# Two state tiles instead of three to TensorE's sum, a third full-size adding DMA, twelve state tiles, and products spread over the steps

## The reference, cut to what matters

```python
u = silu(causal_conv4(xc) + b_conv)          # xc, res = x @ W_in.T, 1024 channels each
dt, B, C = split(u @ W_xproj.T)              # 32, 16, 16
delta = softplus(dt @ W_dt.T + b_dt)
h_t = exp(delta_t * A) * h_(t-1) + delta_t * B_t * u_t     # 1024 channels x 16 states
y_t = sum over the 16 states of h_t * C_t
out = ((y + u * D) * silu(res)) @ W_out.T
```

## Time and profile before

| what | us |
|---|---|
| median of the runs | 2595.19 |
| the profiled execution, its span | 2590.08, 2588.0 |
| TensorE (PE) busy | 2419.2, 93% |
| VectorE (DVE) busy | 1823.6, 70% |
| GpSimd (POOL) busy | 1747.3, 68% |
| ScalarE (ACT) busy | 1442.7, 56% |

### The profile page before, as it was taken

The page is one execution under the profiler, slowest core; times in us unless marked ns, Lnnn a source line. Parts: engine busy times, 40 slices in busy tenths (PEclk is TensorE's granted clock), DMA queues, the critical chain, the costliest instruction groups (busy, mean ns, idle before and its releaser), DMA issues. The chain is left out here.

```text
span 2588.0 us, 38968 instructions
## 1 busy us (share of the span) xinstructions
PE 2419.2 (93%) x15744; PEld 1445.4 (56%) x15744; DVE 1823.6 (70%) x2154; ACT 1442.7 (56%) x2200; POOL 1747.3 (68%) x976
## 2 busy tenths in 40 slices
PE   6899999999999999999999998787999999999997
PEld 3465666665666666666666666543455554554543
DVE  3887897898798799789789878751465455355443
ACT  3577577667667757757757766631333433333332
POOL 0799898999999989989989999960332233143130
PEclk9999999999999999999999999998999999999998
DMA  4767866956866876786695685745000000000000
GB/s 140 191 129 144 223 143 132 235 130 150 218 137 143 190 178 139 163 204 139 142 238 131 140 210 124 155 87 205 1 1 33 33 22 12 33 33 1 17 17 17
DMA packets 158834, 309.23 MB, mean 119 GB/s; under 512 B 39232, under 2 KB 102208, under 8 KB 136000
## 3 DMA queue, kind: packets, MB, share of 16 engines
q0 software_dynamic: 27648, 167.78, 33.3%
q1 hardware_dynamic: 131008, 138.97, 16.3%
HBM read 119.57 MB, written 19.37 MB: 54 GB/s over the span
## 5 line engine op out<-in xcount | busy, mean ns | idle before, releaser
L851 POOL TENSOR_TENSOR mamba_ring<-mamba_ring,mamba_c_row 128x1024 f32<-128x1024 f32 x512 | 1268.1, 2552 | 98.2 <-DVE mamba_ring L748 94.8
L748 DVE TENSOR_TENSOR_SCAN mamba_ring<-mamba_ring,ps 128x512 f32<-128x512 f32 x1024 | 1179.4, 1203 | 189.1 <-PE ps L394 166.7
L602 ACT ACTIVATE mamba_ring<-mamba_delta,mamba_a_neg 128x512 f32<-128x512 f32 x1024 | 658.7, 712 | 85.5 <-DMA mamba_ring<-mamba_ring 84.4
L394 PEld LDWEIGHTS ps<-mamba_diag_b,mamba_v_t 64*128 64x128 f32 x8192 | 500.6, 188 | 291.8 <-issue 208.4
L394 PE MATMUL ps<-mamba_diag_b,mamba_v_t 64*128 64x128 f32 x8192 | 588.0, 285 | 45.7 <-DVE mamba_ring L748 44.3
L298 PE MATMUL ps<-mamba_xt,mamba_wu 128*128 128x512 f32 x512 | 253.4, 623 | 30.1 <-DMA mamba_wu<-w_u 16.1
L1519 POOL TENSOR_TENSOR xf_pr<-xf_pr,xf_top 128x1232 f32<-128x1232 f32 x32 | 75.0, 2343 | 277.2 <-DVE xf_top L1437 277.2
L356 PE MATMUL ps<-mamba_xt,mamba_wres 128*128 128x512 f32 x512 | 252.1, 615 | 0.0
L417 PE MATMUL ps<-mamba_ident,mamba_ring 128*128 128x128 f32 x1536 | 186.3, 278 | 23.6 <-DMA mamba_ring<-mamba_ring 23.5
L867 POOL DMA_DIRECT2D mamba_ring<-mamba_ring x192 | 175.1, 912 | 42.2 <-POOL mamba_ring L851 37.6
L1512 POOL TENSOR_TENSOR xf_xn<-xf_xn,xf_bo_s 128x512 f32<-128x512 f32 x32 | 39.5, 1268 | 222.8 <-PE xf_ps L1089 222.8
(11 more groups left out here) (114 smaller groups left out, 2939.5 us busy)
## 6 DMA issues: line engine op xcount, KB each, us to landing
mamba_ring<-mamba_ring POOLq DMA_DIRECT2D x128, 1024.0 KB, 7.8
mamba_c_row<-c_rows SPq DMA_DIRECT2D x32, 1024.0 KB, 12.2
mamba_ring<-mamba_ring POOLq DMA_DIRECT2D x64, 512.0 KB, 7.2
mamba_wu<-w_u SPq DMA_DIRECT2D x64, 256.0 KB, 3.1
mamba_wres<-w_res SPq DMA_DIRECT2D x64, 256.0 KB, 2.9
mamba_diag_b<-b_diagonals SPq DMA_DIRECT2D x56, 256.0 KB, 8.0
mamba_xt<-x_t SPq DMA_DIRECT2D x8, 1024.0 KB, 8.4
mamba_xres<-x SPq DMA_DIRECT2D x32, 256.0 KB, 4.3
```

The lines of the kernel that those rows point to most:

```text
L394: m = nc.tensor.matmul(ps[:, 2 * s + i, tb * P:(tb + 1) * P], v_t[g % 2][i * H:(i + 1) * H, tb * P:(tb + 1) * P], diag_b[i * H:(i + 1) * H ...
L602: a = nc.scalar.activation(ring[:, q % NR, i, :], delta[:, d, :], ACT.Exp, scale=a_neg[:, d, 2 * k + i:2 * k + i + 1])
L748: m = nc.vector.tensor_tensor_scan(ring[:, r, i, :], ring[:, r, i, :], both[:, bass.ds(i, T, 2)], 0.0, ALU.mult, ALU.add)
L851: nc.gpsimd.tensor_tensor(ring[:, q % NR], ring[:, q % NR], c_row[:, 2 * k:2 * k + 2, :], ALU.mult).then_inc(c_done, 1)
```

## The change

- `merge`: the third adding DMA sums tiles 4, 5 onto 6, 7 (1024 KB) and is issued at k = 1 of the next block; `SUMS` is (6, 7), summed at k = 6 of the next block, both behind `merged[2]`.
- The ring has twelve tiles, delta four blocks instead of eight; `DECAYS` gives its orders for k anew.
- y's transposes are at k = 7, `take_y` at k = 0 and the gating at k = 1 of the block after; v is made at k = 0.
- The parts of the gate, x and output products are spread over other steps, `dt_pair` goes to k = 2, the gate's and u's activations mostly to k = 0 of the next block, softplus to k = 3; `out_second` takes a list of blocks, uses other banks, and waits, adds and norms are moved with it. `dt_pair`, `v_transposes` and `u_product` get the waits that go with the new places (mostly not shown: `y_taken`, `vt_ready`, `delta_ready`, `z2_done`).

The diff, cut to its core; in the steps of TensorE and ScalarE the old lines are left out (they are in the functions above). `delta[:, d, :]` becomes `delta[:, d % EARLY, :]` in `softplus`, `decay` and `make_v`.

```diff
     NG = NB * ND
     TOTAL = NG * NU
     AHEAD = 3
-    DECAYS = ((3,), (), (4,), (5,), (6,), (7, 8), (9,), (10,))
+    DECAYS = ((3,), (4,), (5,), (6,), (7,), (), (8, 9), (10,))
     EARLY = 4
     FIRST_U = (0, 2, 4, 5, 6)
     TWO_U = (0, 1, 4)
     MOST = (5, 5, 6, 6)
-    NR = 10
+    NR = 12
     MERGES = 3
-    SUMS = (4, 5, 7)
-    FREED_BY_MERGE = {0: 0, 1: 0, 2: 1, 3: 1, 6: 2}
-    NEEDS_MERGE = {4: 1, 5: 1, 7: 2}
+    SUMS = (6, 7)
     NSUM = len(SUMS)
     BANK_A, BANK_B = 6, 7
...
         gate = [sb(f"gate{i}", [P, T]) for i in range(2)]
-        delta = sb("delta", [P, ND, T])
+        delta = sb("delta", [P, EARLY, T])
         diag_b = sb("diag_b", [P, TT, NU, H, 2])
         c_row = sb("c_row", [P, NS, T])
...
             def dt_pair(b, d):
-                if d == 4:
-                    pe.wait_ge(vt_ready, b * ND + 4)
-                    pe.wait_ge(y_taken, b * ND + 2)
-                elif d == 6:
-                    pe.wait_ge(y_taken, b * ND + 3)
-                    pe.wait_ge(vt_ready, b * ND + 5)
-                elif b >= 1 and d == 0:
-                    pe.wait_ge(xdbl_ready, b + 1)
-                    pe.wait_ge(y_taken, (b - 1) * ND + 5)
-                    pe.wait_ge(vt_ready, (b - 1) * ND + 7)
-                elif b >= 1:
-                    pe.wait_ge(vt_ready, (b - 1) * ND + 8)
-                    pe.wait_ge(y_taken, (b - 1) * ND + 6)
+                if b >= 1 or d >= EARLY:
+                    g = b * ND + d - 2
+                    pe.wait_ge(y_taken, g - 1)
+                    pe.wait_ge(vt_ready, g + 1)
+                    if d == 0:
+                        pe.wait_ge(xdbl_ready, b + 1)
+                    if d == 4 and b >= 1:
+                        pe.wait_ge(z2_done, (b - 1) * TT + 1)
                 for t0 in (0, T // 2):
                     for i in range(2):
...
                         pe.wait_ge(y_taken, g - 1)
-                    if d == 2:
-                        pe.wait_ge(delta_ready, b * ND + 5)
-                    elif d == 3:
-                        pe.wait_ge(delta_ready, b * ND + 8)
-                    elif d in (5, 6) and b + 1 < NB:
-                        pe.wait_ge(delta_ready, (b + 1) * ND + (2 if d == 5 else 3))
-                pe.wait_ge(merged[NEEDS_MERGE[k]], 16 * (g + 1))
+                    if d % 2 == 1 and (d != 5 or b + 1 < NB):
+                        pe.wait_ge(delta_ready, min(b * ND + d + 5, NG))
+                    if d in (1, 2) and b >= 1:
+                        pe.wait_ge(z2_done, (b - 1) * TT + 2 * d - 1)
+                pe.wait_ge(merged[MERGES - 1], 16 * (g + 1))
                 r = (g * NU + k) % NR
                 for i in range(2):
                     for tb in range(TT):
...
-                if k == 3 and g >= 1:
+                if k == 6 and g >= 1:
                     for e in SUMS:
                         state_sum(g - 1, e)
                 if k == 4 and g + 1 < NG:
...
                         u_product(n, BANK_A, [2 * k, 2 * k + 1])
                     if k in (4, 5) and d in TWO_U:
                         u_product(n + 1, BANK_A, [2 * k - 8, 2 * k - 7])
                 if feeds and d == 5:
+                    if k in (0, 1):
+                        x_product(b + 1, [2 * k, 2 * k + 1])
                     if k in (4, 5):
                         x_product(b + 1, [2 * k - 4, 2 * k - 3])
                     if k == 7:
                         b_columns(b + 1)
+                if d in (0, 4):
+                    if k == 3:
+                        res_product(g, [0, 1])
+                    if k == 7:
+                        res_product(g, [2, 3])
+                if d in (1, 5, 7):
+                    if k == 2:
+                        res_product(g, [0, 1])
+                    if k == 3:
+                        res_product(g, [2, 3])
+                if d in (2, 3):
+                    if k == 3:
+                        res_product(g, [0, 1])
+                    if k == 4:
+                        res_product(g, [2])
+                    if k == 7:
+                        res_product(g, [3])
+                if d == 6:
+                    if k == 5:
+                        res_product(g, [0, 1])
+                    if k == 7:
+                        res_product(g, [2, 3])
+                if (d, k) == (5, 7):
                     out_first(b, 0, [0, 1])
+                if d == 6:
+                    if k == 0:
+                        out_first(b, 0, [2, 3])
+                    if k == 1:
+                        out_first(b, 1, [0, 1])
+                    if k == 2:
+                        out_first(b, 1, [2])
+                    if k == 3:
+                        out_first(b, 0, [4])
+                        out_first(b, 1, [3])
+                    if k == 4:
+                        out_first(b, 1, [4])
+                if d == 7:
+                    if k == 0:
+                        out_first(b, 2, [0, 1])
+                    if k == 1:
+                        out_first(b, 2, [2, 3])
+                    if k == 4:
+                        out_first(b, 2, [4, 5])
+                    if k == 5:
+                        out_first(b, 3, [0, 1])
+                    if k == 7:
+                        out_first(b, 3, [2, 3, 4])
                 if back and (d, k) == (0, 0):
+                    out_first(b - 1, 3, [5])
+                if (d, k) == (2, 2):
                     dt_pair(b, 4)
+                if (d, k) == (4, 2):
                     dt_pair(b, 6)
+                if feeds and (d, k) == (6, 2):
                     dt_pair(b + 1, 0)
+                if back and (d, k) == (0, 2):
+                    dt_pair(b, 2)
+                if back and (d, k) == (1, 6):
+                    pe.wait_ge(vt_ready, g + 2)
+                    out_second(b - 1, 0, y_bank(g), [5])
+                if back and (d, k) == (1, 7):
+                    out_second(b - 1, 0, y_bank(g), [6, 7])
+                if back and (d, k) == (2, 5):
+                    if feeds:
+                        pe.wait_ge(taps, TP * ((b + 1) * ND + 5))
+                    else:
+                        pe.wait_ge(z1_done, b * TT - 1)
+                    out_second(b - 1, 1, BANK_A, [5, 6, 7])
+                if back and (d, k) == (3, 2):
+                    pe.wait_ge(vt_ready, g + 1)
+                    out_second(b - 1, 2, y_bank(g - 1), [6, 7])
                 if back and (d, k) == (3, 5):
                     if feeds:
                         pe.wait_ge(taps, TP * ((b + 1) * ND + 6))
                     else:
+                        pe.wait_ge(z2_done, (b - 1) * TT + 2)
+                    out_second(b - 1, 3, BANK_A, [6, 7])
+                if k == 7 and g >= 1:
+                    y_transposes(g - 1)
             pe.wait_ge(w_loaded, 16 * len(first_loads))
             for j in range(ND):
...
                 g = b * ND + d
                 q = g * NU + k
                 feeds, back = b + 1 < NB, b >= 1
+                m = (b + 1) * ND
+                if k == 7 and g >= 1:
+                    take_yt(g - 1)
+                if k == 0 and d in (1, 2, 3, 4, 5, 7):
+                    take_res(g - 1)
+                    if feeds and d in (2, 3):
+                        silu_u(m + 2 * d - 3)
+                        silu_u(m + 2 * d - 2)
+                    if feeds and d in (1, 4, 5):
+                        silu_u(m + {1: 0, 4: 5, 5: 6}[d])
+                    exp_tables()
+                if k == 4 and d in (5, 7):
+                    take_res(g)
                     if feeds and d == 5:
+                        silu_u(m + 7)
                     exp_tables()
+                if feeds and d < 5:
+                    if k == 2:
+                        last_tap(m + FIRST_U[d], BANK_A)
+                    if k == 6 and d in TWO_U:
+                        last_tap(m + FIRST_U[d] + 1, BANK_A)
+                if k == 3 and d in (2, 4):
+                    for e in (d + 2, d + 3):
+                        softplus(b, e)
+                    exp_tables()
+                if k == 3 and d == 6 and feeds:
+                    for e in (0, 1):
+                        softplus(b + 1, e)
+                    exp_tables()
+                if k == 3 and d == 0 and back:
+                    for e in (2, 3):
+                        softplus(b, e)
+                    exp_tables()
+                if back and (d, k) in ((3, 1), (4, 4)):
+                    rstd_of(b - 1, 2 * d - 6)
+                if back and (d, k) in ((3, 3), (4, 5)):
+                    norm(b - 1, 2 * d - 6)
+                if back and (d, k) in ((3, 4), (4, 6)):
+                    norm(b - 1, 2 * d - 5)
+                if k == 5 and g + 1 < NG:
+                    take_vt(g + 1)
+                if k == 6 and feeds and d == 5:
+                    take_xdbl(b + 1)
                 for ahead in DECAYS[k]:
                     if g * NU + ahead < TOTAL:
...
                 scan(q)
```

(73 more changed lines are left out.)

88 lines of the change are left out of this document (7 added, 81 removed).

## The result

The change makes the kernel slower, by 0.6%: 2611.76 us median (four runs, 2610.63 to 2613.28) against 2595.55, ratio 1.0062 with a 95% interval of [1.0044, 1.0079]. The forecast was 2549, the range 2518 to 2590. The profiled execution's span is 2611.5 us, 23.5 above the one before.

The account below looks back on a forecast made before the run. TensorE's own work was taken as the bound: 197.3 us plus 4.4 idle a row, 7.1 less than 208.8. Six middle periods gave 43 us, start 1, last row 2: 2595.2 - 46 = 2549, range 2518 to 2590.

Parts of the forecast that it names:

- TensorE's tally: TensorE's work a row summed from instruction prices: 202.1 us before, 197.3 after the change.
- idle of 4.4 us a row: TensorE's standing time in a changed middle row: 3.0 us for VectorE's late blocks plus 1.4, in place of 6.8.
- GpSimd: GpSimd's queue: 195.3 us of work a row, 2.0 behind TensorE, with 6 us still to wait in 201.7.
- The gating at k = 1: GpSimd's gating of y a block later: output products use y gated two and three steps before, so no wait.
- The fuller queue: DMA queue: 21.5 us more a row, DMA share 0.86; 0 to 4 us possible, nothing taken beside the 1.4.
- Rival D: Sums at k = 6 wait for the third adding DMA as queue load stretches landings: slower, 2624; chance 0.11.
- D's sign of 4 us a row: Evidence against the forecast: state sums waiting for the adding DMA above 4 us a row and landings above 10.
- Rival E: GpSimd, not TensorE, is the bound and takes the sums' saving at once: little comes, 2590; chance 0.04.
- The last row and the end: Last row 2 us faster from freed GpSimd waits; the very end, with a larger last DMA, 0 +- 3.
- six middle rows: Middle of the pass: each period 7.1 us shorter, 201.7 instead of 208.8, together 43 us.
- ScalarE's moves: Gate and silu at k = 0: up to 1.2 us of VectorE in three blocks, bounds 0 and 4 us a row.
- ScalarE's ring waits: ScalarE's waits for free ring tiles, 84.4 us in the whole pass before, were to be gone.

Follow-up runs that it names:

- e6: Changed kernel with the old reduction put back (third adding DMA 512 KB at k = 7, sums of tiles 4, 5 and 7); ratio to before 0.9918.
- e9: Changed kernel with one state sum, of tile 7, instead of two (tile 6 left out); ratio to before 1.0036.
- e3: Kernel before with one edit: GpSimd gates y at k = 7 instead of k = 6, behind the second adding DMA; ratio to before 1.0033.
- e8: Changed kernel with GpSimd gating only the first 128 of 512 columns of y; ratio to before 0.9937.
- e2: Changed kernel with its third adding DMA moving one tile of two (512 KB instead of 1024); ratio to before 0.9899.

## Why the prediction was wrong, by its own steps

- **TensorE's tally** was right to about 1%. In the changed kernel TensorE works 0.943 of 209.8, 197.9 us a row, beside the 197.3 of the tally. For e6 the tally gives 204.7 of work, and the measured row of 204.7 holds 2.6 of idle. That TensorE's waits for scans would fall was right too: they are 8.8 us from 255 to 1270 us, and 21.7 before. The idle of 4.4 us a row was forecast for a kernel that TensorE bounds; in e6, which it does bound, it is 2.6, and in the changed kernel 11.9.
- **GpSimd** is the step that failed. Its work was taken as 195.3 us a row with "6 us to wait" left, and the only prices of the third DMA were its issue and TensorE's sums; GpSimd's own waits for the adding DMAs were put at nothing, without a reason. They measured 14.9 us a row. The wait that stands ahead of each issue after the first was in the diff (`merged[p - 1]`) and in the old code (`merged[0]`), and I never asked what was queued behind it. A block of GpSimd without such a wait is 24.2 us of work, from the multiplies of k = 2 to those of the next block in the trace after:

```profile
656.45 5.24 POOL L881 TENSOR_TENSOR mamba_ring<-mamba_ring,mamba_c_row 128x1024 f32<-128x1024 f32 x2
...
680.62 5.07 POOL L881 TENSOR_TENSOR mamba_ring<-mamba_ring,mamba_c_row 128x1024 f32<-128x1024 f32 x2
```

That is 193 a row; with 72.2 us of waits in 4.84 rows (255 to 1270 us), 14.9 a row, it comes to 208, and the row is 209.8. TensorE's 197 then is not the bound, and the sum that it saved is mostly off the path: in e9 one sum more brings 7 us.

- **The gating at k = 1** was costed at nothing because y is ready in time. It also was 1.4 us of work that covered the first DMA's landing; e3 prices the same move in the kernel before at 0.33%, with a later gating for TensorE in it.
- **The fuller queue** was sized a little high: 21.5 us a row, where 38.7% of 2611.5 against 33.3% of 2588.0 makes 18.6; the DMA share is 0.82 beside my 0.86. It was then charged to TensorE's sums only, with 0 to 4 us. The sums in fact waited 35.1 us in 4.84 rows, 7.3 a row, and GpSimd's 14.9 were not thought of. The median landing of 7.9 hides it: it is the long ones (up to 14.0) that meet the wait. Rival D named this load, at the sums and with average landings above 10.6 us. The sums' waits passed D's sign of 4 us a row, the median landing did not come near its 10, and the kernel was slower all the same: D had the direction and the load right, and missed GpSimd's queue, which e8 and e9 put on the path.
- **Rival E**, GpSimd as the bound, had 0.04 and a time of 2590, with nothing for GpSimd's waits; its bound was right and its time 22 us short. I had its 195.2 in hand and 197.3 beside it; with two bounds 1% apart the lighter one deserved the same look at its waits.
- **The last row and the end**: forecast 2 us faster and 0 +- 3, measured 23.1 slower to the start of the last sums. The waits of GpSimd make most of it and the chain at the tail the rest. Beside this miss of some 25 us stands that of the six middle rows, 43 us faster by the forecast and 5.7 slower in fact.
- **ScalarE's moves** cost little: the taps' waits for ScalarE are 43.2 us instead of 38.9 in the whole pass, and the ring no longer delays scans (0.6 us, 20.7 before). The forecast that ScalarE's ring waits would be gone failed: they rose from 84.4 to 264.1 us. They are lead and not loss, since hardly a scan waits for ScalarE.

What is not settled: how the 42 us of e2 divide between shorter landings in GpSimd's queue and the shorter waits of TensorE (86.8 to 55.4), since they fall together. GpSimd's place as the bound rests on e8 and e9, of which e8 won back three fifths of what it took off and e9 ran at a lower clock. The spreading and the ring of twelve were not run apart from each other.

## What to carry to other kernels

A wait in front of an issue is paid by everything behind it in that engine's queue; list, for every transfer that depends on another, the work between the issue and the wait, and set it against the longest landing and not the median. When work is taken from the bound engine, look first at the waits of the engine that is 1% behind it. Work moved out of a stretch may have been the cover of a wait that it has nothing to do with.

## What was unexpected

A DMA share up from 0.73 to 0.82 did not move the median landing of the DMAs that GpSimd issues (7.8 to 7.9 us), while two of the loads that SP issues beside them took about twice as long (diagonals 8.0 to 15.5, xt 8.4 to 18.9 us) and C's rows a third longer (12.2 to 16.1).
